# Raw rows copied memory to memory, another order in the first sequence, W1 and the first gathers laid over buffers of the recurrence

## The reference

```python
xn = _layernorm(x)
s  = _L0_attn_ref(xn, ...)             # RWKV block: ln0, ln1, time mix, wkv scan, Wo, ln2, channel mix
g  = _silu(_L0_ffn_ref(xn, Wg, W1, W2))  # 8 experts, each an MLP 256 -> 512 -> 256 with gelu
return x + s * g

# _L0_attn_ref, after x = _ln(x) and h = _ln(x):
k, v, sr = xk @ Wk.T, xv @ Wv.T, sigmoid(xr @ Wr.T)     # xk = h*tmk + shift(h)*(1-tmk), ...
att = _wkv(-exp(time_decay), time_first, k, v)          # a recurrence over the 512 tokens
x = x + (sr * att) @ Wo.T
h2 = _ln(x);  kf = square(relu(xk2 @ Wfk.T))            # 256 -> 1024
return x + sigmoid(xr2 @ Wfr.T) * (kf @ Wfv.T)

# _L0_ffn_ref: probs = softmax(xt @ Wg); every expert picks its 1024 best tokens; a token goes to
# the expert that picked it (else to its own best); out = prob * (gelu(xt @ W1[e]) @ W2[e])
```

## Time and profile before

| | |
|---|---|
| median of 3 runs | 1156.54 us (1156.45, 1156.54, 1160.71) |
| the profiled execution, its own time | 1161.18 us |
| its span, first to last instruction | 1159.4 us |
| mean granted TensorE clock | 0.975 |
| busy share of the span: TensorE, weight loads, VectorE, ScalarE, GpSimd | 91%, 72%, 76%, 54%, 31% |

### The profile page before, as it was taken

One profiled execution on the slowest core, in us unless ns is written; L12 is line 12 of the kernel. 1 busy time (PEld: TensorE's weight loads), 2 busy tenths in 40 slices (PEclk: granted clock), 3 DMA queues, 4 the chain that ended last, 5 costly groups with the idle time before them and its releaser, 6 DMA issues.

```text
span 1159.4 us, 19493 instructions
## 1 busy us (share of the span) xinstructions
PE 1060.0 (91%) x5152; PEld 839.0 (72%) x5153; DVE 877.5 (76%) x1988; ACT 629.0 (54%) x1085; POOL 360.2 (31%) x403
## 2 busy tenths in 40 slices
PE   5559999999999999999998798989889999999997
PEld 5247787776777767767775567667769888888886
DVE  4788888989889888898898968786416666666664
ACT  1538484775857758568583557648234334334332
POOL 2134213011000100010000446364316556555553
PEclk9969999999999999999998899999899999999999
DMA  9334231101101011010110101050143233333220
GB/s 321 114 120 133 93 98 47 56 1 55 37 17 54 0 54 54 0 54 17 37 55 0 44 12 55 1 164 20 62 153 92 94 96 96 98 98 93 90 74 15
DMA packets 60055, 80.44 MB, mean 69 GB/s; under 512 B 7775, under 2 KB 47328, under 8 KB 60003
## 3 DMA queue, kind: packets, MB, share of 16 engines
q1 hardware_dynamic: 48658, 54.69, 14.6%
q0 software_dynamic: 11360, 25.32, 7.3%
HBM read 56.78 MB, written 26.49 MB: 72 GB/s over the span
## 4 chain that ended last, share of the span: by engine, by line
PE 58%; DVE 13%; ACT 12%; issue 10%; POOL 4%; DMA 1%; SPq 0%; DVEq 0%; ACTq 0%; POOLq 0%
PE psKV L869 13%; PE psM L937 12%; PE psM L809 10%; PE psM L948 5%; PE psR L948 5%; DVE arena L1268 3%; ACT arena L594 3%; PE psM L821 2%; ACT arena L598 2%; POOL sorted_list L401 2%; PE psT L774 2%; PE psT L927 2%; PE psR L730 1%; PE psM L839 1%; PE psM L846 1%
## 5 line engine op out<-in xcount | busy, mean ns | idle before, releaser
L869 PE MATMUL psKV<-arena 128*128 128x256 f32 x1024 | 237.6, 387 | 3.0 <-ACT arena L598 1.4
L869 PEld LDWEIGHTS psKV<-arena 128*128 128x128 f32 x1024 | 195.2, 194 | 42.8 <-issue 14.8
L809 PE MATMUL psM<-arena 128*128 128x512 f32 x384 | 174.4, 601 | 6.6 <-DVE arena L1268 5.6
L408 POOL TENSOR_SCALAR lnw<-mv 128x4 f32<-128x4 f32 x32 | 11.6, 361 | 496.6 <-DVE mv L1249 496.3
L937 PE MATMUL psM<-arena 128*128 128x128 f32 x1152 | 144.2, 279 | 0.1
L937 PEld LDWEIGHTS psM<-arena 128*128 128x128 f32 x1152 | 135.7, 193 | 4.1 <-issue 1.8
L684 ACT ACTIVATE arena<-arena,info_t 128x256 f32<-128x256 f32 x72 | 43.2, 600 | 169.1 <-DVE info_t L1469 169.1
L809 PEld LDWEIGHTS psM<-arena 128*128 128x128 f32 x384 | 70.7, 192 | 87.9 <-issue 86.3
L460 POOL DMA_INDIRECT out_dram<-arena,out_idx x72 | 88.4, 1228 | 97.6 <-DVE row_idx L1464 83.8
L508 ACT ACTIVATE arena<-s_ring,cf 128x256 f32 (+1 forms) x128 | 66.3, 590 | 79.0 <-POOL cf L413 79.0
L1268 DVE SCALAR_TENSOR_TENSOR arena<-arena,vecs 128x512 f32<-128x512 f32 x160 | 108.7, 746 | 0.0
(11 more groups left out here) (191 smaller groups left out, 2012.7 us busy)
## 6 DMA issues: line engine op xcount, KB each, us to landing
desk<-in_x SPq DMA_DIRECT2D x16, 512.0 KB, 4.9
arena<-in_x SPq DMA_DIRECT2D x16, 512.0 KB, 3.6
desk<-in_xT SPq DMA_DIRECT2D x16, 512.0 KB, 4.7
xs_rows<-arena SPq DMA_DIRECT2D x16, 512.0 KB, 3.0
xs_rows<-s_ring SPq DMA_DIRECT2D x16, 512.0 KB, 3.0
desk<-in_W SPq DMA_DIRECT2D x8, 512.0 KB, 7.9
arena<-in_W SPq DMA_DIRECT2D x8, 512.0 KB, 7.9
out_dram<-arena,out_idx POOLq DMA_INDIRECT x72, 2.8
```

The lines of the kernel that those rows point to most:

```text
L809: ins = pe.matmul(psM[:, u % 3, :], w[:, k, c * P:(c + 1) * P], mixA[:, m, k, :], start=(k == 0), stop=(k == CH - 1))
L869: ins = pe.matmul(psKV[:, j // 2, (j % 2) * C:(j % 2 + 1) * C], kf2[:, h, j * P:(j + 1) * P], wfv[:, h, :], start=(h == 0), stop=(h == HC ...
```

## The change

1. SP no longer stores x_in. `copy_x(b)` copies the rows of x straight from the input to `xs_rows`, memory to memory (512 KB each, in runs of 1 KB): copy b-5 in round b from round 5 on, and the last five one after another behind `store_s(NB-3)`, ahead of the load of the sorted list. `norm0` waits for the load of `x_in` in place of the store.
2. First sequence, ScalarE: `affine1(0)` stands ahead of the wait for the weights and the copy L657; `norm0(1)` stands between the first and the second pair of `take_kvr(0)`. TensorE: two routers, `turn1(0)`, two routers, `project`, in place of four routers and then `turn1(0)`. VectorE: `statistics(2)` stands behind `moments1(0)`; the part of `prepare` that touches the weights stands behind `wkv_start(0)`.
3. Rounds 0 and 1, VectorE: the second `extra` stands ahead of `wkv_mix` in place of behind it.
4. `dmix` and `kx` move behind `att` in the arena. W1 then lies over mixA, kvs, E1, E2, and the gathered rows over qb, pp, lb, all of them dead at the last `att_done`. So SP's load of W1 waits for `att_done`; GpSimd clears the rows in round 15, behind its scatters and ahead of `rstd2(15)`.
5. Round 15: TensorE's `project_out` stands ahead of `channel_out(14, 1)`. VectorE waits for the sorted list and takes six indices and three infos (`first_indices`) between `residual1` and `mix2`; before, that stood behind `residual2(14)`. ScalarE's squares of sequence 15 go between the relus, the last two behind `sigmoid_fr`.
6. Seam: TensorE turns tiles 0 and 1 between `channel_out(15, 1)` and `channel_out(15, 2)`; VectorE prepares the inputs of tiles 0 and 1 ahead of `gate_out(15)`, and that of tile 2 behind `residual2(15)`. The steps begin at 0 in place of -3 on these two engines.

The diff, cut to its core:

```diff
         mixA = part(3 * CH * SEQ)...
-        dmix = part(CH * SEQ)...
...
-        kx = part(CH * SEQ)...
...
         att = part(CH * SEQ)...
+        dmix = part(CH * SEQ)...
+        kx = part(CH * SEQ)...
...
             def load_x(b):
                 sp.dma_start(x_in, xrows[:, ds(b * J, J), :]).then_inc(S["x_in"], 16)
-                store_x(b)
-
-            def store_x(b):
-                wait_run(sp, S["x_in"], b * 16 + 16)
-                sp.dma_start(xs_store[:, ds(b * J, J), 0:C], x_in).then_inc(S["x_out"], 16)
+
+            def copy_x(b):
+                sp.dma_start(xs_store[:, ds(b * J, J), 0:C], xrows[:, ds(b * J, J), :]).then_inc(S["x_out"], 16)
...
             load_weights("proj_w_in", (wk, WkT), (wv, WvT), (wr, WrT))
-            store_x(0)
...
                 load_x(b)
                 store_s(b - 3)
+                copy_x(b - 5)
...
             store_s(NB - 3)
+            for b in range(NB - 5, NB):
+                copy_x(b)
 
             sp.wait_ge(S["list_scattered"], 16 * NTILE)
...
-            sp.wait_ge(S["mix2_done"], NB)
-            sp.wait_ge(S["mixr2_done"], NB)
+            sp.wait_ge(S["att_done"], CH * NB)
...
+            def zero_rows():
+                pool.wait_ge(S["att_done"], CH * NB)
+                for i in range(RING):
+                    ins = pool.memset(rows[i], 0.0)
+                ins.then_inc(S["rows_zeroed"], 1)
...
+                if not ahead:
+                    zero_rows()
                 rstd2(b)
...
                 wait_run(act, S["fetched"], b + 1)
-                wait_run(act, S["x_out"], 16 * b + 16)
+                wait_run(act, S["x_in"], 16 * b + 16)
...
             norm0(0)
             norm1(0)
+            affine1(0)
             act.wait_ge(S["weights_in"], 16 * 4)
             act.activation(wfk_hi[:], wfk, ACT.Copy).then_inc(S["wfk_hi_done"], 1)
-            affine1(0)
-            take_kvr(0, 0, 4)
+            take_kvr(0, 0, 2)
+            norm0(1)
+            take_kvr(0, 2, 4)
             exponents(0, 0)
             exponents(0, 1)
             exps(0)
-            norm0(1)
...
-            relus(NB - 1, *range(HC))
-            squares(NB - 1, *range(HC))
+            relus(NB - 1, 0, 1)
+            for h in range(2, HC):
+                squares(NB - 1, h - 2)
+                relus(NB - 1, h)
             sigmoid_fr(NB - 1)
+            squares(NB - 1, HC - 2, HC - 1)
...
-                if ffn:
+                if ffn and ahead:
                     channel_out(b - 1, 1)
                 project_out(b)
+                if not ahead:
+                    channel_out(b - 1, 1)
...
-            for n in range(4):
-                router(n, n, n // 2)
+            router(0, 0, 0)
+            router(1, 1, 0)
             turn1(0)
+            router(2, 2, 1)
+            router(3, 3, 1)
...
+            turn_x(0, 0)
+            turn_x(1, 1)
+            channel_out(NB - 1, 2)
+            channel_out(NB - 1, 3)
...
+            mlp_in(0, 0)
+            steps(pe, step, 0)
...
+                else:
+                    extra(b, 1)
                 wkv_mix(b)
-                extra(b, 1)
+                if not (isinstance(b, int) and b < 2):
+                    extra(b, 1)
...
+            def first_indices():
+                v.wait_ge(S["list_in"], 16)
+                for t in range(RING):
+                    take_index(t, t)
+                for t in range(3):
+                    take_info(t, t)
+                v.tensor_scalar(s_idx[:], list_sb[:, 0:RING, 0], 2.0, 1.0, ALU.mult, ALU.add
+                                ).then_inc(S["s_idx_ready"], 1)
...
                 extra(b, 2)
                 if ahead:
                     wkv_start(b + 1)
+                else:
+                    first_indices()
                 extra(b, 3)
                 mix2(b)
...
             fetch(0)
             statistics(1, 1, 0)
-            statistics(2, 0, 1)
             embed_scale(0)
             embed_shift(0)
             moments1(0)
+            statistics(2, 0, 1)
             statistics(3, 1, 1)
+            decay_parts()
             mix1(0)
-            prepare()
             v.wait_ge(S["pow_ready"], 16)
             fetch(1)
             wkv_start(0)
+            prepare()
...
+            v.wait_ge(S["w1_in"], 16 * E)
+            mlp_input(0, 0)
+            mlp_input(1, 1)
             gate_out(NB - 1)
             residual2(NB - 1)
-            v.wait_ge(S["w1_in"], 16 * E)
-            steps(v, step)
+            mlp_input(2, 2)
+            take_info(3, 3)
+            steps(v, step, 0)
```

58 lines of the change are left out of this document (23 added, 35 removed).

## The result

| | before | after |
|---|---|---|
| median of 6 runs each | 1160.53 us (1156.45 to 1163.47) | 1146.43 us (1145.82 to 1148.25) |
| the profiled execution, its span | 1161.18, 1159.4 us | 1145.82, 1144.0 us |
| ratio of the times | 1 | 0.9881, 95% interval 0.9862 to 0.9900 |

The account below looks back on a forecast made before the run. TensorE bounds rounds and experts, so gains come only where it starves: the start and the seam. 9.1 + 4.3 = 13.4 us off a median of 1156.5 gives 1143.1 us, range 1138 to 1151.

Parts of the forecast that it names:

- The store: First sequence: without the wait on the store norm0(0) starts at 11.0 for 16.91, project(0) at 30.5 for 36.34, 5.8 us.
- Routers late next: First sequence: the two routers left behind turn1(0), 7.0 us, end at 30.5 and are what then holds project(0).
- Round 0 and GpSimd: Round 0: GpSimd's scale is ready before wkv_mix(0), so mix1(1) starts at 64.7 for 74.94, 10.2 us.
- Rival B: Round 0: GpSimd misses the 2.1 us gap and stays starved; start worth 4.1, in all 8.4, time 1148; chance 0.12.
- What round 1 inherits: Start, as passed on to round 1: between 8.8 and 10 us sooner, taken as 9.1.
- Rival D: Start: TensorE's matmuls in project(0) no longer start slow, 1.7 us more, time 1141; chance 0.05.
- The copies and the list: Rounds and round 15: copies cost nothing in the rounds; five ahead of the list cost 0 to 3 us, taken as nothing.
- Rival E: Round 15: five slow memory-to-memory copies make the list late; over 0.5% slower if it lands at 845 or later, 1163; chance 0.04.
- Round 15: Round 15: project_out(15) 2.0 us sooner and turn2 at full clock, 1.0 for 1.97; 3.0 us in all.
- The seam: Seam: mlp_in(0) 7 us sooner, but s of sequence 15 limits tile 4 to 5.8; less 1.5 for slow clock, 4.3 us.
- Rival C: Seam gives nothing because the list, the clearing or s is late next: 9.1 us alone, time 1147.5; chance 0.12.
- Rival F: Whole kernel: copies or moved loads disturb rounds, or several setbacks meet; 5 us or less remain, 1152 to 1156; chance 0.05.

Follow-up runs that it names:

- the last kernel: Changed kernel with both project(0) ahead of routers 2 and 3 and the last squares ahead of sigmoid_fr(15): median 1142.00 us, ratio 0.9870.

## Why the prediction was right, and where it was off

**The kernel's bound and the two places.** Right: a steady round is 47.5 us in both, and all the gain is in the start and the seam.

**The absolute time.** The measured median is 3.3 us over the forecast. That is the baseline, not the change: the forecast stood on 1156.54, the median of three runs shown, and six runs gave 1160.53. Off that, 13.4 us would have been 1147.1, 0.7 from the result. The range held. Read by the traces the gain was 15.4 and not 13.4, and the 2 us more are the start's (below).

**The store.** `norm0` at 11.0 (measured 11.00), `turn1` ended at 23.5 (23.55), `project(0)` at 30.5 (30.03). The experiment with the store puts 5.3 to 6.0 us on it, out of the 5.8 named.

**Routers late next.** Right, and the experiment that moved them behind `project` took 2.9 us more of that.

**Round 0 and GpSimd.** The forecast had L411 at 1.01 us, `mix1(1)` at 64.7; measured 1.01 and 63.62. Rival B, GpSimd still starved, did not come, and the experiment that made it come priced it: 4.2 to 4.5 us to round 4, where the forecast had 10.2 - 6.4 = 3.8 for this step. Here row and rule stood against each other. The Trainium skill (SBUF — State Buffer, Who interferes with whom) lets the loser wait until the other's instruction ends; the same four GpSimd instructions took 10.0 us beside a run of `wkv_mix` and 1.8 beside batch statistics, so here the trace disagrees with it: the loser waits through a run of instructions. The rule would have left the distance at `mix1(1)` at 6.4 us; measured were 11.3. But not every run does this. In the changed kernel's first sequence GpSimd works on the router's numbers beside the six instructions of `mix1(0)`, back to back and with two inputs in SBUF each:

```profile
25.67 4.06 DVE L1282 SCALAR_TENSOR_TENSOR arena<-arena,vecs 128x512 f32<-128x512 f32 x6
25.91 0.58 POOL L380 TENSOR_SCALAR desk<-desk 128x12 f32<-128x12 f32 x1
26.57 0.59 POOL L382 TENSOR_TENSOR desk<-desk,info 128x12 f32<-128x12 f32 x1
```

In the kernel before, where VectorE was idle beside them, these two took 0.21 and 0.22 us. They lose less than one VectorE instruction (0.68 us) each, as the rule has it. What makes `wkv_mix` different, whose instructions follow each other every 0.60 us, no run shows.

**The term that was mis-sized** is "What round 1 inherits is between 8.8 and 10; I take 9.1". It measured 10.3 at the first `hidden` and 11.7 at round 2 (11.4 at round 15). One microsecond is the sum of small steps: `wkv_state(0)` came at 42.77 for 43.6, because the second k product was in at 35.83 for 36.4 and `wkv_start` ended at 39.1 for 39.7. The other 1.3 us came in round 1, and I had nothing for it. Stretches of three microseconds beside or just behind the first `hidden` show it, of the kernel before, of the one after, and of the experiment with the second `extra` behind `wkv_mix` again:

```profile
98.00:101.00 3.00, 3.00 (x9) 2.35 (x8) 3.00 (x3) 0.89 (x2) 3.00 (x1) 0.50 0.20 79
```
```profile
88.00:91.00 3.00, 3.00 (x15) 2.49 (x14) 3.00 (x4) 2.23 (x4) 2.84 (x3) 1.00 0.18 70
```
```profile
90.00:93.00 3.00, 2.86 (x7) 2.31 (x8) 1.98 (x4) 1.64 (x2) 2.68 (x5) 0.50 0.46 159
```

TensorE is busy without a break in the first two, but at a granted 0.50 (1.2 GHz) before, with 9 matmuls, and at 1.00 (2.4 GHz) after, with 15. Ahead of it TensorE had idled more in the kernel before. By the starts of its matmuls the slow stretch of the kernel before lasts from 97.91 to 101.25, and the same eight matmuls take 1.8 us in the kernel after: 1.5 us lost. The experiment settles which part of the change this belongs to. From the first `hidden` to the second scan of round 2 are 68.0 us in the kernel before and 68.1 in that experiment, both with the slow stretch, and 66.7 in all the others that have the unedited order of `extra` and `wkv_mix`. So part 3 wins this 1.3 us too. That it does so through the idle time ahead of `hidden` is argued and not shown.

**Rival D.** It did not come. `project(0)` took 12.03 us for 12.21, and its first products were again 0.85 us apart, though TensorE had worked without a break from 21.58.

**The copies and the list.** Right to cost nothing: 325 GB/s of copied bytes, near the store's rate that I had taken from the earlier trace rows, and done 4 us ahead of the list's issue. Rival E falls as a matter of size: sixteen copies, not five, were needed for the change to come out level. The estimate of 14.7 us took the limit of about 358 GB/s for one core from the Trainium skill (DMA: Bandwidth & Descriptors, Specifications) and added up what is read and what is written, which the page does not say; it has the limit as half of a stack's 716 GB/s. The copies took about 10.6 us (790.4 to 801), and the stretch shown has 325 GB/s copied, which is 650 read and written. So the sum of both did not keep to 358 here.

**Round 15.** Forecast 3.0 us for `project_out` and the clock of `turn2`; measured 2.6 at the first product of `hidden(15)` with `mix_lo` between the two kernels, and 4.3 in the experiment, some 2.1 of them likely by waits of that chip. The squares were forecast to leave 1.7 us behind the last `receptance` (measured idle 1.72), no gain, and they gave none.

**The seam.** Forecast 5.8 us to tile 4 and 1.5 back by the clock, 4.3; measured 17.05 - 11.36 = 5.7 and 1.7 back, 4.0. That the 1.5 back came out right is luck in part, since the clock need not have fallen in the profiled execution: behind an idle time of 2.22 to 2.35 us it fell in four other traces and stayed up in six (see the last section). Gather landing in 2.9 us and `xn(4)` behind `combine(0)`: as forecast. Rival C, the seam gives nothing, did not come on the first chip. On the second, the stall around tiles 3 to 5 took some 3 us (tile 6 turned 79.4 us behind the scan for 76.3), and this stays open: the records of TensorE's instructions end 4 us before its waiters go on. Some of GpSimd's indirect DMAs fall into that stretch, but so they do on the first chip. All eight kernels that ran on that chip show it, the one with the early infos in another place, and none on the two other chips. No run told its cause.

**Rival F**, a change that gives 5 us or less, did not come on either chip that ran the changed kernel: on the second, where less came of it, the medians are still 10.6 us apart.

## What to carry to other kernels

Ask for each wait at the start of a kernel whether it is one for data or for a buffer: a store waited for only so that its source may be overwritten can be made a copy from memory to memory, off every engine's order, provided nobody reads it soon. Ask of each small GpSimd chain what VectorE does beside it; placing it beside batch statistics instead of the run of `wkv_mix` was worth 4.2 to 4.5 us, nearly as much as the removed wait (5.3). 1.3 of these microseconds were a slow stretch of TensorE's clock that went with it. When a seam is tightened, look at what the waiting engine has next in its order: two tiles turned early brought 3.6 us at once and 2 at the end, because s of the last sequence was due soon behind.

## What the runs showed of the hardware that was not expected

GpSimd's starvation is exact: 2.96, 1.05 and 5.59 us in a kernel with other work around it, on another chip. And it is particular to the run of instructions: beside `mix1(0)` GpSimd loses under 0.4 us an instruction.

The clock is not. Behind an idle time of TensorE of 2.30 to 2.35 us ahead of tile 4, `mlp_in(3)` took 3.52 us in the changed kernel, 2.63 on the second chip (and the group behind it 2.92 for 1.89), 3.58 with `project(0)` first, and 2.93 in the last kernel; with all copies at the seam it took 2.99 behind 2.22 us. It took 1.95, full clock, in that with the squares first, and 1.95 or 1.96 in five others, all on the second chip: with `extra` behind, with the store, with the routers first, with `project_out` behind, with W1 late. Each time that the clock fell, 1.6 to 1.7 us were lost to tile 5. The same seam can so be 1.7 us apart by that alone; on the second chip the stall behind it swallowed the difference (11.9 to 12.0 us from tile 4 to tile 6 either way).

The start of `project(0)` is uneven too, and the granted clock, which reads 1.00, does not explain it: 12.03 to 13.59 us for the same 24 matmuls, and with it most of the 1.7 us of spread at `wkv_state(0)`.

Copies of 512 KB from memory to memory ran about as fast as the store of the same size from SBUF (some 300 GB/s by the earlier trace rows): 325 GB/s with five in a row, and 349 with sixteen in the stretch shown, which has loads of W1 in it.
